# A cross-attention and expert kernel: order of the last batch, split of W2 in the second blocks, and output banks

## The reference

```python
x = x + tanh(g_xattn) * attention(ctx, layernorm(x))        # softmax over 375 + 112 keys, 8 heads
xn = layernorm(x)
P = softmax(xn @ Wg); mask = top2(P); P_norm = P * mask / (sum(P * mask) + 1e-9)
h = gelu(einsum('bsd,edf->ebsf', xn, W1) + b1)              # E = 8, D = 256, F = 1024
y = einsum('bsd,bse->bsd', einsum('ebsf,efd->ebsd', h, W2) + b2, P_norm)
out = x + tanh(g_ffn) * y
```

## Time and profile before

| | us |
|---|---|
| median of 3 runs (lowest to highest) | 440.5 (439.67 to 443.6) |
| the profiled execution | 443.38, of which 441.6 is the span from the first to the last instruction |
| busy in the span | PE 399.2 (90%), DVE 272.0 (62%), ACT 236.1 (53%), POOL 199.5 (45%) |
| granted PE clock, mean of the span | 0.968 of full |

### The profile page before, as it was taken

One profiled execution on the slowest core, in us unless ns is written; L12 is line 12 of the kernel. 1 busy time (PEld: TensorE's weight loads), 2 busy tenths in 40 slices (PEclk: granted clock), 3 DMA queues, 4 the chain that ended last, 5 costly groups with the idle time before them and its releaser, 6 DMA issues.

```text
span 441.6 us, 8655 instructions
## 1 busy us (share of the span) xinstructions
PE 399.2 (90%) x2786; PEld 329.8 (75%) x2786; DVE 272.0 (62%) x705; ACT 236.1 (53%) x556; POOL 199.5 (45%) x291
## 2 busy tenths in 40 slices
PE   1689989999998989999899989889979999999982
PEld 1678746776676767667676768776979999999982
DVE  4663755748567585856755483642657687787660
ACT  2532236766758566675856442431655566575640
POOL 2442016566555656655567023140457564424332
PEclk9999988999999999999999696999998999999998
DMA  7401000010100001000001148034997988959232
GB/s 236 126 1 35 0 20 17 2 36 1 36 0 13 25 0 59 0 0 1 0 2 34 35 149 269 13 120 150 272 374 185 333 251 240 316 151 359 50 38 24
DMA packets 30838, 43.91 MB, mean 99 GB/s; under 512 B 2401, under 2 KB 25985, under 8 KB 30800
## 3 DMA queue, kind: packets, MB, share of 16 engines
q1 hardware_dynamic: 25904, 37.61, 25.4%
q0 software_dynamic: 4192, 5.80, 6.9%
q10 hardware_dynamic: 704, 0.03, 0.1%
HBM read 38.54 MB, written 4.89 MB: 98 GB/s over the span
## 4 chain that ended last, share of the span: by engine, by line
PE 60%; POOL 12%; DVE 10%; issue 9%; ACT 3%; DMA 3%; DVEq 1%; POOLq 1%; ACTq 0%
PE ph L1860 6%; PE sc L1331 5%; PE pt L1339 5%; PE po L1356 4%; PE pk L1185 3%; PE py L2138 3%; POOL krow L520 3%; POOL krot L510 3%; POOL krot L514 3%; PE py L2139 3%; PE py L2140 3%; PE pk L1186 2%; PE pk L1187 2%; DMA xt<-rows_scratch,xi 2%; PE py L2126 2%
## 5 line engine op out<-in xcount | busy, mean ns | idle before, releaser
L1918 POOL DMA_INDIRECT out<-yv,xi x21 | 38.8, 1845 | 75.8 <-DMA out<-yv,xi 31.0
L1955 ACT ACTIVATE hf<-ph,b1t 128x128 f32<-128x128 f32 (+1 forms) x128 | 41.6, 398 | 55.3 <-PE ph L1860 27.9
L1029 DVE TENSOR_REDUCE negmax<-sc 112x1 f32<-112x487 f32 x64 | 39.5, 660 | 50.9 <-PE sc L1331 50.9
L805 ACT COPY probt<-pt 125x448 f32<-125x448 f32 x64 | 34.3, 537 | 43.5 <-PE pt L1339 43.5
L797 ACT ACTIVATE prob<-sc,negmax 112x487 f32<-112x487 f32 x64 | 42.2, 664 | 27.4 <-DVE negmax L1029 27.0
L1356 PEld LDWEIGHTS po<-probt,vals 125*64 125x64 f32 (+1 forms) x512 | 26.8, 145 | 21.4 <-issue 16.0
L1339 PEld LDWEIGHTS pt<-ident,prob 112*125 112x125 f32 x256 | 36.7, 197 | 7.2 <-DVE prob L1039 3.1
L1339 PE MATMUL pt<-ident,prob 112*125 112x112 f32 x256 | 40.4, 284 | 0.6 <-DVE prob L1039 0.6
L633 POOL TENSOR_TENSOR cl<-cf,ch 128x500 fp32r<-128x500 f32 (+1 forms) x16 | 15.9, 994 | 48.4 <-ACT ch L747 48.4
L1331 PE MATMUL sc<-keys,queries 64*112 64x488 f32 x128 | 36.2, 644 | 0.6 <-ACT keys L765 0.6
L1356 PE MATMUL po<-probt,vals 125*64 125x112 f32 (+1 forms) x512 | 33.9, 277 | 0.7 <-ACT heads L813 0.4
(11 more groups left out here) (352 smaller groups left out, 1095.9 us busy)
## 6 DMA issues: line engine op xcount, KB each, us to landing
w_first<-in_L_ffn_W SPq DMA_DIRECT2D x10, 1024.0 KB, 8.4
w_next<-in_L_ffn_W SPq DMA_DIRECT2D x10, 1024.0 KB, 8.8
w_third<-in_L_ffn_W SPq DMA_DIRECT2D x8, 1024.0 KB, 9.5
ctx_t<-in_ctx SPq DMA_DIRECT2D x8, 375.0 KB
w_first<-in_L_xattn_Wkv SPq DMA_DIRECT2D x1, 1024.0 KB, 9.7
x_all<-in_x SPq DMA_DIRECT2D x2, 448.0 KB, 4.1
out<-x_all SPq DMA_DIRECT2D x1, 896.0 KB, 5.2
rows_scratch<-x SPq DMA_DIRECT2D x1, 672.0 KB, 4.2
```

The source lines that it names most:

```text
L1029: dve.tensor_reduce(negmax[:, h % 2:h % 2 + 1], sc[h % 2][0:M, 0:JA], AX, ALU.max, negate=True).then_inc(max_done.sem, 1)
L1918: pool.indirect_dma_start(out=out, out_offset=bass.IndirectOffsetOnAxis(ap=xi[:, i, n:n + 1], axis=0), in_=yv[:, i % KEPT, n, :], in_offse ...
L1955: last = act.activation(hf[:, n % 3, c], ph[n % 3][:, c], ACT.Gelu, bias=b1t[:, bass.ds(owner_of * FB + (count * g + u), 1)])
```

## The change

- **PE, last batch.** `logits` and `sum_columns` of group 0 move from the end of the seventh batch to behind the last batch's second pair of scores. `scores` of the last pair moves ahead of `values(last, 0)`. `list_rows` of group 0 moves behind the transposes of heads 6 and 7.
- **DVE, last batch.** `find` moves along, behind two row maxima. `output(before, 0)`, `invert_pair(last, 4)` and both `lanes` come ahead of `pick`. `weigh` of group 0 moves behind the last row maxima. `output(before, 1)` and `finish_early` come ahead of `pick_next`. For the late groups `weigh` and `spread` move behind `lines`.
- **POOL.** `output_rstd(before)` moves ahead of the first gather.
- **Experts.** `plain` ends at tile 1, so tiles 2 and 3 split W2; W2 loads of later tiles then wait for the split and not for `down`. From tile 4 on the outputs of odd tiles go to the bank `pm[0]`, and `down` waits for `out_rows` of two tiles before. `turn_rows(2)` and `turn_shares` move behind `down` of the group (0, 1).

```diff
--- before.py
+++ after.py
@@ -680,8 +680,8 @@
                 pool.wait_ge(router.share_done, 1)
                 router.spread(pool, router.pool_steps, GROUPS[0])
                 pool.wait_ge(score_done.sem, score_done.at(*last, H))
+                output_rstd(*before)
                 beside["gather"](pool, 0)
-                output_rstd(*before)
                 beside["gather"](pool, 1)
                 keep_x1(*before)
                 router.lines(pool, router.pool_steps, NEXT)
@@ -1090,11 +1090,6 @@
                         invert_pair(*following, 0)
                 prepare_beside(prepare, h, 1, following, after)
                 late_output(t, p, h, previous)
-                if following and not after:
-                    if h == 7:
-                        dve.wait_ge(router.tables_set, TABLES)
-                        dve.wait_ge(router.summed, 1)
-                        router.find(dve, logits_of, GROUPS[0])
 
             def place(n):
                 router.place(dve, slot_sums[:, GROUPS[n]], n)
@@ -1122,31 +1117,33 @@
 
                 row_max(*last, 2)
                 row_max(*last, 3)
+                dve.wait_ge(router.tables_set, TABLES)
+                dve.wait_ge(router.summed, 1)
+                router.find(dve, logits_of, GROUPS[0])
                 router.mark(dve, 0)
                 router.carry(dve, 0)
+                invert_pair(*last, 2)
                 dve.scalar_tensor_tensor(wg_c[:], column_sums.rearrange("q (a e) -> q a e", a=1)
                                          .broadcast_to([P, KD, E]), -1.0 / D, wg_t[:], ALU.mult, ALU.add) \
                     .then_inc(centred, 1)
-                invert_pair(*last, 2)
                 row_max(*last, 4)
                 row_max(*last, 5)
                 place(0)
                 router.split(dve, 0)
                 router.blocks(dve, 0)
+                output(*before, 0)
+                invert_pair(*last, 4)
+                router.lanes(dve, 0, slice(0, 1), GROUPS[0])
+                router.lanes(dve, 0, slice(1, 2), GROUPS[0])
                 beside["pick"](dve, early_sums)
-                output(*before, 0)
+                row_max(*last, 6)
+                row_max(*last, 7)
                 router.weigh(dve, gates, GROUPS[0], 1)
                 dve.sem_inc(router.share_done, 1)
-                invert_pair(*last, 4)
-                router.lanes(dve, 0, slice(0, 1), GROUPS[0])
-                row_max(*last, 6)
-                row_max(*last, 7)
-                router.lanes(dve, 0, slice(1, 2), slice(0, 3))
-                router.lanes(dve, 0, slice(1, 2), slice(3, 6))
+                invert_pair(*last, 6)
+                output(*before, 1)
+                router.finish_early(dve, list_sums)
                 beside["pick_next"](dve)
-                invert_pair(*last, 6)
-                router.finish_early(dve, list_sums)
-                output(*before, 1)
                 output(*before, 2)
                 last_output(*last, 0)
                 dve.wait_ge(logit_done, 7)
@@ -1162,13 +1159,13 @@
                 router.find(dve, logits_of, GROUPS[LAST])
                 router.mark(dve, LAST)
                 last_output(*last, 2)
-                router.weigh(dve, gates, slice(GROUPS[NEXT].start, B), LAST + 1)
-                router.spread(dve, router.step, slice(GROUPS[NEXT].start, B))
                 place(LAST)
                 router.split(dve, LAST)
                 router.blocks(dve, LAST)
                 router.lanes(dve, LAST, slice(0, 2), GROUPS[LAST])
                 router.lines(dve, router.step, LAST)
+                router.weigh(dve, gates, slice(GROUPS[NEXT].start, B), LAST + 1)
+                router.spread(dve, router.step, slice(GROUPS[NEXT].start, B))
                 router.finish(dve, list_sums)
                 beside["plan"](dve)
 
@@ -1390,15 +1387,6 @@
                         pe.wait_ge(tokf_done, 1)
                         pe.wait_ge(x2_done.sem, x2_done.at(t, p, 0))
                         turn(2, x2, (4, 5))
-                        pe.wait_ge(tokf_done, 2)
-                        pe.wait_ge(vals_done.sem, vals_done.at(*following, JT))
-                        pe.wait_ge(small_loaded, 4 * 16)
-                        for b in range(4):
-                            logits(b, wg_t)
-                        pe.wait_ge(tokf_done, 3)
-                        logits(4, wg_t)
-                        logits(5, wg_t)
-                        sum_columns()
 
             def turn(n, rows, batches):
 
@@ -1463,6 +1451,12 @@
 
                 transpose_probs(*last, 0)
                 scores(*last, 1)
+                pe.wait_ge(tokf_done, 3)
+                pe.wait_ge(vals_done.sem, vals_done.at(*last, JT))
+                pe.wait_ge(small_loaded, 4 * 16)
+                for b in range(6):
+                    logits(b, wg_t)
+                sum_columns()
                 transpose_probs(*last, 1)
                 values(*before, 3)
                 scores(*last, 2)
@@ -1471,18 +1465,17 @@
                 transpose_probs(*last, 2)
                 project_output(*before)
                 transpose_probs(*last, 3)
+                scores(*last, 3)
                 values(*last, 0)
-                scores(*last, 3)
                 transpose_probs(*last, 4)
                 transpose_probs(*last, 5)
                 values(*last, 1)
-                pe.wait_ge(router.lanes_done, 3)
+                transpose_probs(*last, 6)
+                transpose_probs(*last, 7)
+                pe.wait_ge(router.lanes_done, 2)
                 pe.wait_ge(router.lines_done, 2)
-                pe.wait_ge(exp_done.sem, exp_done.at(*last, H - 1))
                 list_rows(0, 0, range(6))
                 list_rows(0, 1, range(6))
-                transpose_probs(*last, 6)
-                transpose_probs(*last, 7)
                 values(*last, 2)
                 values(*last, 3)
                 pe.wait_ge(x2_done.sem, x2_done.at(*last, 0))
@@ -1505,13 +1498,13 @@
                 beside["up"](pe, 0, 1)
                 pe.wait_ge(router.early_found, 2)
                 pe.matmul(list_sums, ident[:], router.early_sums[:], start=True, stop=False)
-                pe.wait_ge(router.lanes_done, 4)
+                pe.wait_ge(router.lanes_done, 3)
                 pe.wait_ge(router.lines_done, 4)
                 list_rows(NEXT, 0, range(1))
                 list_rows(NEXT, 1, range(1))
                 place(LAST)
                 beside["up"](pe, 1, 0)
-                pe.wait_ge(router.lanes_done, 5)
+                pe.wait_ge(router.lanes_done, 4)
                 pe.wait_ge(router.lines_done, 6)
                 list_rows(LAST, 0, range(1))
                 list_rows(LAST, 1, range(1))
@@ -1649,11 +1642,15 @@
 
         def plain(i):
 
-            return i < EARLY
+            return i < PICKED
 
         def split_before(i):
 
-            return GROUPS_BEFORE[max(i, EARLY)] - GROUPS_BEFORE[EARLY]
+            return GROUPS_BEFORE[max(i, PICKED)] - GROUPS_BEFORE[PICKED]
+
+        def banks(i):
+
+            return py if i < EARLY or i % 2 == 0 else pm[:1]
 
         def tile_of_group(n):
 
@@ -1681,10 +1678,9 @@
                 sp.wait_ge(up_done, GROUPS_BEFORE[user + 1])
             sp.dma_start(raw1[r][:], w1[bass.ds(e, 1)].rearrange("a k f -> (a k) f").rearrange("(k p) f -> p k f", p=P)) \
                 .then_inc(w1_loaded[r], 16)
-            if n >= RING and plain(user):
-                sp.wait_ge(down_done, GROUPS_BEFORE[user + 1])
-            if n >= RING and not plain(user):
-                sp.wait_ge(w2l_done, 2 * (user - EARLY + 1))
+            if n >= RING:
+                sp.wait_ge(down_done, GROUPS_BEFORE[PICKED])
+                sp.wait_ge(w2l_done, 2 * (user - PICKED + 1))
             sp.dma_start(raw2[r][:], w2[bass.ds(e, 1)].rearrange("a f d -> (a f) d").rearrange("(f p) d -> p f d", p=P)) \
                 .then_inc(w2_loaded[r], 16)
 
@@ -1948,7 +1944,7 @@
                     if plain(before):
                         act.wait_ge(down_done, n - 2)
                     else:
-                        act.wait_ge(hl_done, n - 2 - GROUPS_BEFORE[EARLY])
+                        act.wait_ge(hl_done, n - 2 - GROUPS_BEFORE[PICKED])
                 count, rows = chunks_of(i), rows_of(i)
                 for u in range(count):
                     c = slice(u * rows, (u + 1) * rows)
@@ -1969,7 +1965,7 @@
                     return
                 if n == 0:
                     act.wait_ge(w2_loaded[raw_of(i)], loaded(i))
-                    if i >= EARLY + 2:
+                    if i >= PICKED + 2:
                         act.wait_ge(down_done, GROUPS_BEFORE[i - 1])
                 c = slice(n * FB // 2, (n + 1) * FB // 2)
                 act.copy(w2h[i % 2][:, c], raw2[raw_of(i)][:, c]).then_inc(w2h_done, 1)
@@ -2046,7 +2042,7 @@
                 if plain(i):
                     return
                 c = slice(n * FB // 2, (n + 1) * FB // 2)
```

(25 more changed lines are left out.)

## The result

| | before | after |
|---|---|---|
| median of 4 runs each, us (lowest to highest) | 442.05 (439.67 to 445.05) | 452.79 (451.42 to 453.04) |
| profiled execution, and its span | 443.38, 441.6 | 453.0, 451.3 |
| granted PE clock, mean of the span | 0.968 | 0.949 |

The ratio is 1.0242 (95% interval 1.0189 to 1.0295): 2.4% slower, some 10.7 us. The forecast was 443.9, with a range up to 448. Executions of one kernel differ with the granted clock (before took from 438.28 us at a mean of 0.984 to 448.74 at 0.956), and each trace is of one execution.

A forecast was written before the change was run, and what follows sets the result against it. It took PE as the late bound and, earlier, the routing chain and a DRAM chain through the x_all store. Terms 0.4 + 0.9 + 1.6 + 1.5 - 1.0 = +3.4 on the 440.5 median gave 443.9, range from just above 436.3 to 448.

The forecast's parts named there:

- Term 1: Early lists and first two gathers: the first up starts later, +0.4 us (-0.8 to +2.7).
- Term 2: Late groups' shares behind the lines: their store releases the third gather later, +0.9 us (0.2 to 1.5).
- Term 3: turn_rows(2) behind down(0, 1): nothing itself, but PE's waits lower the clock, +1.6 us (0 to 3.2).
- Term 4: Split of tiles 2 and 3: PE's third bias waits for add_bias, +1.5 us (-1.0 to +1.5).
- Rival (b): Slower: PE's clock also falls at the wait of Term 4, 445.5 us; chance 0.12.
- Term 5: Two output banks for later tiles: PE's waits on the bank go, -1.0 us (-0.6 to -2.3).
- (a): Slower: the second weight load delays the second gather, which takes 7.3 to land, 446.2 us; chance 0.17.
- (d): Faster: earlier W2 loads finish before gathers 5 and 6, ending PE's waits in 330 to 335, 436.3 us; chance 0.10.

The follow-up runs named there:

- lists_back: The changed kernel with the early lists again ahead of the transposes of heads 6 and 7: 451.58 us, ratio 1.021 against before.
- lists_pick_back: The changed kernel with the early lists ahead of the transposes again and pick and pick_next in their old places: 448.34 us, ratio 1.0113 against before.
- experts_only: The kernel before with the changed expert part alone: 443.79 us, ratio 1.0013.
- experts_mended: experts_only with turn_rows(2) again ahead of down(0, 1) and both add_bias ahead of tile 2's second split_hidden: 438.79 us, ratio 0.9942 against before.
- banks_alone: The kernel before with only the two sets of output banks added: 439.95 us, ratio 0.9947.
- lists_alone: The kernel before with only the early lists moved behind the transposes of heads 6 and 7: 445.92 us, ratio 1.0071.
- logits_alone: The kernel before with only logits, column sums and find moved behind the last batch's scores of head 1: 443.96 us, ratio 1.0011.
- weigh_alone: The kernel before with only the weighing of group 0 moved behind the last row maxima: 442.34 us, ratio 0.9997.
- lists_pick_weigh_back: The changed kernel with early lists, picks and weighing of group 0 all put back: 444.42 us, ratio 1.0058 against before.
- filled: lists_pick_back plus five unused 512-column matmuls in the place of PE's wait for the first gathers: 445.68 us, ratio 1.005 against before.
- pick_alone: The kernel before with only pick moved behind the last lanes and pick_next behind finish_early and output(before, 1): 445.81 us, ratio 1.008.
- lists_weigh_back: The changed kernel with early lists ahead of the transposes and group 0 weighed ahead of invert_pair(4) again: 448.85 us, ratio 1.012 against before.
- logits_back: The changed kernel with logits, column sums and find ahead of the second scores again: 452.23 us, ratio 1.016 against before.
- lists_and_pick: The kernel before with two moves, early lists behind the transposes and later pick and pick_next: 449.97 us, ratio 1.0146.
- attn_only: The changed kernel's attention part with the expert part of before: 453.81 us, ratio 1.0245 against before.
- three_back: lists_weigh_back with logits, column sums and find put back as well: 449.17 us, ratio 1.0129 against before.

## Why the prediction was wrong

**Term 1 failed: +0.4 (at most +2.7) was forecast, +8.0 is what the first `up` lost, +9.5 the second.** Three of its steps broke.

- "From there to the last `invert_pair` DVE does what it did before." DVE does, but PE does not: with PE at half clock from 250 to 260, DVE waits 1.85 for the places that PE adds up and 3.10 for the projection, and the last pair begins at 267.09, not 264.2. That puts the lists at 269.23, not 265.2 to 265.9. I had moved DVE's work as if PE would deliver on the old times.
- The lists kept their 3.44 in my sum. PE stood 2.17 for the scaling ahead of the transposes, and the lists, right behind these, ran 5.25. They did so in all five traces that have them there; in the others they took 2.86 to 5.13.
- The second weight load was seen to be late, and its collision priced at a landing of 5.0. Since the lists were later than forecast, it left at 277.09, between the two gathers (271.3 forecast); the second gather took 6.4 to land and was awaited for 1.50, and then the `up` itself took 1.5 more, at half clock, which stood in no term.

By experiments, of the 2.4% the late lists cost 0.71% alone, the late picks 0.80%, and both together 1.46%. With both put back in the changed kernel 1.13% (0.57% to 1.69%) stays, and its cause is open: with the weighing back as well 0.58% is left, with PE's wait filled 0.50%, but neither step is clear of the noise, and the late weighing costs nothing alone. The sentence that the share store "shifts by about as much, because `weigh` is later" passed over that the store would meet the first weight load, which the same change makes late: 4.0 to land before, 6.2 after. The Trainium skill's rule cited there (DMA: Bandwidth & Descriptors, "Issuing engines are not separate DMA queues") bears on this store too: 6.3 beside the load in lists_back, 2.0 in lists_pick_back, where the load had left at 258.00, 7.8 ahead of it.

**Term 2 held.** The third gather was released by the share store, 2.0 behind `where` instead of 1.0: +1.0 for +0.9.

**Term 3 held in kind.** PE stands 0.78 and 1.92 (1.0 and 1.9 forecast). The clock behind it cost 1.0 in the changed kernel (3.03 for 2.02) and nothing in experts_only (2.02), inside the range of 0 to 3.2. That it is a matter of clock after a wait was right; that the same would happen ahead of the first `up` was not seen. The Trainium skill (TensorE: Matmul & The Clock Gate, "HAM oscillation — how this bites in real kernels") says so of waits for data between the bursts of a loop; the traces here agree for some waits (3.55 behind 1.50 in after) and not for others (2.02 behind 1.92 in experts_only).

**Term 4 held**: 1.39 of wait for 1.5. Rival (b), the clock behind it, shows too: the `up` right behind took 3.63 in after and 3.18 in experts_only, and 2.05 in experts_mended; 1.6 was forecast for it. Undoing terms 3 and 4 brought 0.7% (1.0013 to 0.9942), 3.1 as forecast for the two. That the sum fits is in part luck: the intervals of the two ratios overlap, and in the trace of experts_only term 3's clock cost nothing while rival (b)'s cost 1.1.

**Term 5 held in kind and may be too small**: -1.0 forecast, -0.53% alone, which is -2.3 (-0.7 to -4.0), the end of my range, with the forecast inside the interval. I had counted only 0.4 of the last tile's 1.7, because the last `add` waits for the one before it; but the adds before it came earlier too, the third from the end by 3.2 in the trace of banks_alone, counted from the scores near 240.

**The rivals.** (a) had the right place and the wrong size: 446.2, from one gather's landing, which came out at 6.4. None of them had the lists 4.5 late, or PE at half clock ahead of them. The sum of the expert terms 3 to 5 was +2.1; +0.6 (-1.2 to +2.3) was measured. Two slips in the arithmetic do not change this: the upper ends add up to +8.3, not +7.7, and (d)'s 436.3 lies above the 436.1 below which most of it was put.

## What to carry to other kernels

When work is moved in an order by hand, carry the new times through every engine that takes part: the durations of the engine that feeds the moved step may change with it, here PE's, by a factor of two. A gain ahead of a wait on a transfer can be worth nothing, as in lists_back: price a wait of PE by the slower groups behind it too, and look for a step that can stand in its place. Test the parts of a bundled change one by one; here the part with the gain (the banks) was hidden under a reorder that cost more than four times as much.

## What was not expected of the hardware

What the `up` groups behind PE's wait for the first gathers took, over the kernels run (L1831 and its like, then the two `up` groups of 16 matmuls):

| kernel | PE's wait for gathers, us | first `up`, us | second `up`, us |
|---|---|---|---|
| before, lists_alone, logits_alone, weigh_alone, banks_alone, lists_pick_weigh_back, filled | none | 2.02 | 2.03 |
| experts_only, experts_mended | 0.15, 0.32 | 2.02 | 2.03 |
| pick_alone | 0.70 | 2.02 | 2.03 |
| lists_weigh_back | 1.20 | 2.02 | 2.03 |
| after | 1.50 | 3.55 | 2.03 |
| logits_back | 1.52 | 3.76 | 3.76 |
| lists_and_pick | 2.29 | 3.75 | 3.76 |
| attn_only | 1.47 and 1.36 | 3.47 | 2.03 |
| three_back | 2.92 | 3.36 | 2.03 |
| lists_pick_back | 2.92 | 3.75 | 3.70 |
| lists_back | 5.74 | 3.75 | 3.76 |

The same 16 matmuls take 2.0 or up to 3.8 by what PE did ahead of them. The length of the wait alone does not settle it: three_back and lists_pick_back waited 2.92 both, and only the second has two slow groups. And a busy share is not a clock: from 250 to 260 of after PE is busy 10.00 of 10.00 us, at a granted clock of 0.50.
